# Channel attention: part of the sum of exponentials moves from TensorE to accumulating DMAs

## The reference

```python
q = jnp.einsum('bchw,oc->bohw', x, w_q)
kwin = _unfold2d(kmap, 7)     # 49 shifted windows of the padded keys, plus rel_h or rel_w
vwin = _unfold2d(vmap, 7)
attn = jax.nn.softmax(q[..., None] * kwin, axis=-1)   # over the 49 taps
out = jnp.sum(attn * vwin, axis=-1)                   # each channel by itself
```

## Time and profile before

| what | value |
|---|---|
| runs of the kernel | 8085.47, 8098.6, 8104.42 us; median 8098.6 |
| span of the profiled execution | 8087.0 us |
| instructions | 141762 |
| mean granted TensorE clock | 0.979 |

### The profile page before, as it was taken

The page is one execution under the profiler, slowest core; times in us unless marked ns, Lnnn a source line. Parts: engine busy times, 40 slices in busy tenths (PEclk is TensorE's granted clock), DMA queues, the critical chain, the costliest instruction groups (busy, mean ns, idle before and its releaser), DMA issues. The chain is left out here.

```text
span 8087.0 us, 141762 instructions
## 1 busy us (share of the span) xinstructions
PE 7551.7 (93%) x55106; PEld 6507.3 (80%) x55106; DVE 5845.1 (72%) x8981; ACT 3601.8 (45%) x6912; POOL 4566.7 (56%) x2002
## 2 busy tenths in 40 slices
PE   5999998999997998799999999999999999997999
PEld 4777776789997775588888888888888888886899
DVE  5666665334442555798998999999999989996664
ACT  3556554333332332345445454545545454554222
POOL 3555552033331001588777887878878787886232
PEclk9999998999998999899999999999999999998999
DMA  3111114855557772100000000000000000002452
GB/s 144 57 60 66 56 62 137 277 152 146 148 146 215 220 206 85 25 19 19 24 21 21 18 18 26 18 20 19 20 27 18 15 21 24 23 12 79 144 163 81
DMA packets 633017, 617.20 MB, mean 76 GB/s; under 512 B 465525, under 2 KB 498421, under 8 KB 627174
## 3 DMA queue, kind: packets, MB, share of 16 engines
q1 hardware_dynamic: 581318, 483.44, 21.5%
q0 software_dynamic: 33856, 96.69, 3.3%
q10 hardware_dynamic: 17376, 30.54, 1.0%
HBM read 397.01 MB, written 193.76 MB: 73 GB/s over the span
## 5 line engine op out<-in xcount | busy, mean ns | idle before, releaser
L1892 POOL TENSOR_TENSOR e_ev<-e_se,e_v 128x2048 f32<-128x2048 f32 (+1 forms) x896 | 3307.9, 3712 | 858.9 <-ACT e_se L1845 856.5
L1845 ACT ACTIVATE e_se<-e_stage 128x512 f32<-128x512 f32 x3136 | 1868.5, 598 | 2038.3 <-PE e_stage L1677 1991.5
L1991 DVE SCALAR_TENSOR_TENSOR e_stage<-e_k,e_rl,e_qp 128x512 f32<-128x512 f32 x3136 | 2299.7, 746 | 250.1 <-ACT e_se L1845 199.3
L1684 PE MATMUL e_pe_sum<-e_ident,e_se 128*128 128x128 f32 x12544 | 1888.5, 273 | 16.4 <-ACT e_se L1845 12.2
L1684 PE MATMUL e_pv_sum<-e_ident,e_ev 128*128 128x128 f32 x12544 | 1881.1, 273 | 0.5 <-POOL e_ev L1892 0.5
L1684 PEld LDWEIGHTS e_pe_sum<-e_ident,e_se 128*128 128x128 f32 x12544 | 1556.7, 140 | 261.3 <-ACT e_es L1833 21.8
L1677 PE MATMUL e_stage<-e_top,e_minus 128*128 128x512 f32 x3136 | 1513.4, 483 | 163.1 <-DVE e_stage L1991 160.9
L1684 PEld LDWEIGHTS e_pv_sum<-e_ident,e_ev 128*128 128x128 f32 x12544 | 1483.0, 141 | 205.7 <-issue 203.7
L911 POOL DMA_DIRECT2D agg<-c_ot x384 | 334.6, 874 | 880.6 <-ACT c_ot L989 771.0
L403 POOL TENSOR_TENSOR a_pr<-a_pr,a_rden 128x480 f32<-128x480 f32 x512 | 494.6, 987 | 547.2 <-DVE a_rden L636 547.2
L1677 PEld LDWEIGHTS e_stage<-e_top,e_minus 128*128 128x128 f32 x3136 | 598.2, 191 | 219.6 <-DVE e_stage L1991 185.2
(11 more groups left out here) (175 smaller groups left out, 11663.9 us busy)
## 6 DMA issues: line engine op xcount, KB each, us to landing
qkv<-b_ot SPq DMA_DIRECT2D x120, 512.0 KB, 5.9
c_xt<-qkv SPq DMA_DIRECT2D x384, 160.0 KB, 3.8
agg<-c_ot POOLq DMA_DIRECT2D x384, 160.0 KB, 2.5
f_ws<-in_L_w_sets SPq DMA_DIRECT2D x32, 1152.0 KB, 8.0
a_xb<-in_x SPq DMA_DIRECT2D x24, 768.0 KB, 5.1
a_xr<-in_x SPq DMA_DIRECT2D x32, 512.0 KB, 3.8
x<-a_xr SPq DMA_DIRECT2D x32, 512.0 KB, 2.7
b_xc<-x SPq DMA_DIRECT2D x32, 512.0 KB, 6.0
```

The costliest lines, as they stand in the source:

```text
L1684: last = nc.tensor.matmul(acc[:, c * PART:(c + 1) * PART], lhsT=src[:, c * PART:(c + 1) * PART], rhs=ident[:], is_transpose=True, start=j ...
L1845: nc.scalar.activation(se[(t * K2 + o) % NSE][:, i], stage[:, bank_of(t, j), :], ACT.Exp)\
L1892: nc.gpsimd.tensor_tensor(split(ev[(t * NG2 + g) % NEV][:, 0:size]), split(se[(t * K2 + o) % NSE][:, i:i + size]), window(v[h], h, u, o, i ...
L1991: nc.vector.scalar_tensor_tensor(rows(stage[:, bank_of(t, j), :]), win, rl[:, h, o:o + 1], rows(qp[:]), ALU.add, ALU.mult).then_inc(multip ...
```

## The change

Two accumulators `acc` of four tap tiles (4 x 512 elements on 128 partitions, 1 MB) take turns from tile to tile. ACT writes the exponentials of taps 0 to 3 of row 0 into the accumulator in place of `se`. After POOL has weighed both parts of row 1, it issues a DMA that adds the first four taps of that row (in `se`) onto the accumulator, in SBUF; likewise for rows 2, 3 and 4, each after the one before has landed. PE no longer adds the first four taps of rows 0 to 4 (20 tiles). In place of them it adds the four tiles of the accumulator, one each at taps 44, 45, 46 and 47, after it has waited at tap 44 for the DMA of row 4. So PE adds 33 tiles (29 directly, four gathered) in place of 49; the weighted sums stay as they were. ACT's waits on buffers follow: those for gathered parts wait for the DMA's landing.

```diff
+        acc = [sb(f"acc{u}", [PART, ROW_PARTS[0][1], TPX]) for u in range(2)]
...
+        gathered = sem("gathered")
...
+        GATHERED = (1, 2, 3, 4)
+        NACC = ROW_PARTS[0][1]
+        DIRECT = [j for j in range(NTAP) if j % K2 >= NACC or j // K2 not in (0, *GATHERED)]
+        NES = len(DIRECT) + NACC
+        ACC_AT = (44, 45, 46, 47)
...
+        def exps(t, j, taps=None):
+            o, i = divmod(j, K2)
+            buf = acc[t % 2] if o == 0 and i < NACC else se[(t * K2 + o) % NSE]
+            return buf[:, i] if taps is None else buf[:, i:i + taps]
+        def sums_made(n, t, j):
+            return tiles(n, t, NES, sum(d <= j for d in DIRECT) + sum(a < j + E_LAG for a in ACC_AT))
+        def gathers(n, t, o):
+            return 16 * tiles(n, t, len(GATHERED), sum(r <= o for r in GATHERED))
...
             def sum_exponential(n, t, j, first=False):
-                o, i = divmod(j, K2)
-                if j == 0 and (t or not first):
+                if j == DIRECT[0] and (t or not first):
                     pe.wait_ge(e_taken, tiles(n, t, 1, 0))
                 pe.wait_ge(exp_done, tiles(n, t, NTAP, j + 1))
-                add_up(pe_sum, se[(t * K2 + o) % NSE][:, i], j).then_inc(e_summed, 1)
+                add_up(pe_sum, exps(t, j), j == DIRECT[0], j == DIRECT[-1]).then_inc(e_summed, 1)
+            def sum_gathered(n, t, i):
+                if i == 0:
+                    pe.wait_ge(gathered, gathers(n, t, K2))
+                add_up(pe_sum, acc[t % 2][:, i], False, False).then_inc(e_summed, 1)
...
                 shift(n, t, j)
-                if t * NTAP + j >= E_LAG or not first:
+                if (t * NTAP + j >= E_LAG or not first) and before(t, j, E_LAG)[1] in DIRECT:
                     sum_exponential(n, *before(t, j, E_LAG), first=first)
+                if j in ACC_AT:
+                    sum_gathered(n, t, ACC_AT.index(j))
...
+                if j == 0 and (t >= 2 or not first):
+                    act.wait_ge(e_summed, tiles(n, t - 2, NES, NES))
+                elif i == start and j:
+                    lag = NSE * K2
+                    if part_of(j) == 0 and before(t, j, lag)[1] == 0:
+                        lag *= 2
+                    if t * NTAP + j >= lag or not first:
+                        t0, j0 = before(t, j, lag)
+                        if part_of(j) == 0 and j0 // K2 in GATHERED:
+                            act.wait_ge(gathered, gathers(n, t0, j0 // K2))
+                        else:
+                            act.wait_ge(e_summed, sums_made(n, t0, j0 + size - 1))
+                        act.wait_ge(weighted, tiles(n, t0, NG2, group_of(j0) + 1))
...
+            def gather(n, t, o):
+                if o == GATHERED[0]:
+                    pool.wait_ge(weighted, tiles(n, t, NG2, 1))
+                else:
+                    pool.wait_ge(gathered, gathers(n, t, o - 1))
+                flat = lambda x: x.rearrange("p i n -> p (i n)")
+                pool.dma_start(flat(acc[t % 2][:]), flat(se[(t * K2 + o) % NSE][:, 0:NACC]), accum_op=ALU.add).then_inc(gathered, 16)
...
                     for g in range(NG2):
                         weigh(n, t, g, first=n == 0)
+                        if g % 2 and g // 2 in GATHERED:
+                            gather(n, t, g // 2)
```

More of the change, by code:

```diff
@@ L1569, in bank_lag, with part_of @@
             return 2 if t * NTAP + j in (1, TPB * NTAP - 1) else NST
+        def exps(t, j, taps=None):
[6 more added lines that the diff above has]
+            return 16 * tiles(n, t, len(GATHERED), sum(r <= o for r in GATHERED))
+        def part_of(j):
+            return group_of(j) % len(ROW_PARTS)
         def group_of(j):
@@ L1679, in shift, with add_up @@
                                  skip_group_check=True).then_inc(shifted, 1)
-            def add_up(acc, src, j):
+            def add_up(total, src, opens_, closes):
                 for c in range(NBLK2):
-                    last = nc.tensor.matmul(acc[:, c * PART:(c + 1) * PART], lhsT=src[:, c * PART:(c + 1) * PART],
-                                            rhs=ident[:], is_transpose=True, start=j == 0 and c == 0,
-                                            stop=j == NTAP - 1, skip_group_check=True)
+                    last = nc.tensor.matmul(total[:, c * PART:(c + 1) * PART], lhsT=src[:, c * PART:(c + 1) * PART],
+                                            rhs=ident[:], is_transpose=True, start=opens_ and c == 0,
+                                            stop=closes, skip_group_check=True)
                 return last
             def sum_exponential(n, t, j, first=False):
-                o, i = divmod(j, K2)
-                if j == 0 and (t or not first):
+                if j == DIRECT[0] and (t or not first):
                     pe.wait_ge(e_taken, tiles(n, t, 1, 0))
                 pe.wait_ge(exp_done, tiles(n, t, NTAP, j + 1))
-                add_up(pe_sum, se[(t * K2 + o) % NSE][:, i], j).then_inc(e_summed, 1)
+                add_up(pe_sum, exps(t, j), j == DIRECT[0], j == DIRECT[-1]).then_inc(e_summed, 1)
[3 more added lines that the diff above has]
+                add_up(pe_sum, acc[t % 2][:, i], False, False).then_inc(e_summed, 1)
             def sum_weighted(n, t, j, first=False):
@@ L1704, in sum_weighted @@
                     pe.wait_ge(weighted, tiles(n, t, NG2, g + 1))
-                add_up(pv_sum, ev[(t * NG2 + g) % NEV][:, i], j).then_inc(v_summed, 1)
+                add_up(pv_sum, ev[(t * NG2 + g) % NEV][:, i], j == 0, j == NTAP - 1).then_inc(v_summed, 1)
             def back(n, t, copies=0, near_=0):
@@ L1828, in take_e_sums @@
             def take_e_sums(n, t):
-                act.wait_ge(e_summed, tiles(n, t, NTAP, NTAP))
+                act.wait_ge(e_summed, tiles(n, t, NES, NES))
                 if t > 0 or n:
@@ L1838, in exponential @@
                 start, size = ROW_PARTS[g % 2]
[L1839 to L1843, removed]
+                if j == 0 and (t >= 2 or not first):
[11 more added lines that the diff above has]
+                        act.wait_ge(weighted, tiles(n, t0, NG2, group_of(j0) + 1))
                 act.wait_ge(shifted, tiles(n, t, NTAP, j + 1))
-                nc.scalar.activation(se[(t * K2 + o) % NSE][:, i], stage[:, bank_of(t, j), :], ACT.Exp)\
-                    .then_inc(exp_done, 1)
+                nc.scalar.activation(exps(t, j), stage[:, bank_of(t, j), :], ACT.Exp).then_inc(exp_done, 1)
             def step(n, t, j, first=False, final=False):
@@ L1892, in weigh @@
                 nc.gpsimd.tensor_tensor(split(ev[(t * NG2 + g) % NEV][:, 0:size]),
-                                        split(se[(t * K2 + o) % NSE][:, i:i + size]),
+                                        split(exps(t, o * K2 + i, size)),
                                         window(v[h], h, u, o, i, size), ALU.mult).then_inc(weighted, 1)
+            def gather(n, t, o):
[5 more added lines that the diff above has]
+                pool.dma_start(flat(acc[t % 2][:]), flat(se[(t * K2 + o) % NSE][:, 0:NACC]), accum_op=ALU.add).then_inc(gathered, 16)
             for x in (xb, *k, *v, near, pair):
```

## The result

The changed kernel took 8252.35 us (median), 1.0193 of the kernel before (95% interval 1.0178 to 1.0207): 156 us slower, where 118 us faster was forecast. The time lies inside the stated range, at its upper end; the direction was wrong.

A forecast was written before the change was run, and what follows sets the result against it. Three engines nearly full, PE first: odd tiles PE-bound, even ones not wholly. Odd tiles 2.0 us less, even 1.6: 3.6 to 3.7 a pair over 32 pairs, 118 us off 8098.6, giving 7980 us; range 7,800 to 8,270.

The forecast's parts named there:

- a loop that leaves 57.7 us for an odd tile: From one landing of gather 4 to the next, through PE's wait at tap 44: 57.7 us, 2.0 less than 59.7.
- The removed sums: On PE, 16 of 49 tile sums a tile go: 16 x 0.43 = 6.9 us, 440 us were PE alone the limit.
- POOL then does five rows of taps with three issues: 39.2: Odd tile, POOL's first multiply to the end of row 4: 5 x 7.36 + 2.4 = 39.2 us.
- the sign that POOL's idle on exponentials would shrink by more than half: Listed sign in the stage: POOL's wait for exponentials, 589.5 us between 4000 and 7000 us, shrinks by more than half.
- taps 29 to 34 at 0.66: Even tile, DVE's products after tap 28, at 0.66 us each, put product 34 at 51.6 us after the landing.
- The 43.6 us up to tap 28: Even tile, DVE's first product to that of tap 28: 43.6 us, DVE almost without a gap, unchanged by PE's relief.
- the first product 4.0 after the landing: Even tile, DVE's first product after PE's landing point: 3.2 us before, 4.0 with two gathered sums in the way.
- The half microsecond for the clock: Added to each tile's time, 0.5 us for the granted clock falling after PE's stand at tap 44.
- The landing, D = 6.8 us: Time for a 1 MB gather to land: 6.8 us, by two reads and a little more; bounds 4.0 and 9.2.
- The deciding point, 8.2 us: Landing time over which gathers are too slow, POOL waiting before each of three gathers and PE longer.
- The rival that came true (slower, 0.32): Gathers too slow, landing over 8.2 us; at 9.2 us +5.4 a pair, +173, about 8,270 us; chance 0.32.
- The lost DVE time: DVE's small tensor_scalar locked out by POOL: at most 141 us over 72 instructions, growth likelier, counted in a half microsecond.

The follow-up runs named there:

- no_gathers: The changed kernel without its DMAs and PE's wait for them, the first four taps of rows 1 to 4 left out of the sum: 8036.68 us, 0.9935.
- light DVE: The changed kernel without gathers or their wait, and 24 of 34 instructions of DVE's bounds chain per half band made eight times smaller: 7928.97 us, 0.9798.
- half_bytes: The changed kernel with gathers of two of the four tap tiles, 512 KB in place of 1 MB: 8049.13 us, 0.9952.
- next_tile: The changed kernel with the four gathered sums moved from taps 44 to 47 to taps 2 to 5 of the next tile, copy and inversions later: 7991.5 us, 0.9876.
- rows_2_to_5: The kernel with gathered sums at the next tile's taps 2 to 5, with rows 2 to 5 gathered in place of 1 to 4: 8242.07 us, 1.0184.
- next_tile_no_gathers: The kernel with the four sums at the next tile's taps 2 to 5, without its DMAs and the wait for them: 7953.22 us, 0.9821.

## Why the prediction was wrong

The mechanism that lost the time was in the prediction: the wait at tap 44, in order ahead of the shifts of 45 to 48, the DVE that starves behind it, the clock that falls after a long stand. It stood there as a loop that leaves 57.7 us for an odd tile. PE's stand itself came out as forecast: on the mean 2.9 us in odd tiles, where some 3 were written, and 1.5 in even ones. What failed is the rest of the loop, which was longer than worked out. Here it is in its parts, each the mean of 28 tiles of its kind:

| stretch of the loop, us | forecast | measured |
|---|---|---|
| odd tile: landing to POOL's first multiply | 10.7 | 10.96 |
| from there to the end of row 4 | 39.2 | 43.34 |
| to the landing, issue included | 6.8 | 7.33 |
| even tile: landing to DVE's first product | 4.0 | 5.64 |
| from there to the end of row 4 | 54.9 (58.9 - 4.0) | 58.80 |
| to the landing, issue included | 6.8 | 7.22 |
| allowed for clock and jitter in both | 2.0 | in the rows above |
| pair | 124.4 | 133.3 |

*The removed sums* were counted rightly: 4096 matmuls less. I then let PE's relief reach the end of row 4, in both kinds of tile, and it does not.

*Odd tile, "POOL then does five rows of taps with three issues: 39.2".* This is the step that failed first. It made POOL full from row 0 to row 4. In the odd tile shown, POOL began row 0 at 4987.10 and ended row 4 at 5031.53 (the multiplies of its timeline):

```profile
4987.10 4.19 POOL L1932 TENSOR_TENSOR e_ev<-e_acc,e_v 128x2048 f32<-128x2048 f32 x1 [0.80 <-ACT e_acc L1886]
4991.32 3.19 POOL L1932 TENSOR_TENSOR e_ev<-e_se,e_v 128x1536 f32<-128x1536 f32 x1
4997.09 7.36 POOL L1932 TENSOR_TENSOR e_ev<-e_se,e_v 128x2048 f32<-128x2048 f32 x2 [2.58 <-ACT e_se L1886]
5004.39 0.85 POOL L1943 DMA_DIRECT2D e_acc<-e_se  x1
5005.56 7.38 POOL L1932 TENSOR_TENSOR e_ev<-e_se,e_v 128x2048 f32<-128x2048 f32 x2 [0.32 <-ACT e_se L1886]
5014.96 0.87 POOL L1943 DMA_DIRECT2D e_acc<-e_se  x1 [2.02 <-DMA e_acc<-e_se]
```

That is 44.4 us. In it POOL waited 2.58 for exponentials and 2.02 for its own first gather, which landed later than the median 7.4; another 0.95, for the third, came behind row 4. The kernel before already waited for exponentials in this stretch. In the odd tile of the earlier trace rows POOL began row 0 at 4919.50 and ended row 4 at 4964.33, a third of the way through the 22.09 us from 4956.97: 44.8 us.

```profile
4919.50 7.35 POOL L1892 TENSOR_TENSOR e_ev<-e_se,e_v 128x2048 f32<-128x2048 f32 x2 [0.65 <-ACT e_se L1845]
```

On the mean the stretch took 43.7 us before and 43.3 after; the forecast took all of its waits away. Most of the miss is not the gathers' doing: in no_gathers the stretch still took 41.7, though five rows of multiplies without an issue need 36.8. DVE's work holds part of that: with light DVE it took 40.3. So the sign that POOL's idle on exponentials would shrink by more than half failed too: 589.5 us before, and 461.5 and 43.0 (on `se` and on `acc`) after, 504.5 together.

*Even tile, "taps 29 to 34 at 0.66".* In the even tile shown DVE's product of tap 28 starts at 5088.95 and that of tap 34 at 5096.44: 7.5 us, not 4.0. DVE's timeline has three reductions in it, and PE's the two projections at taps 29 and 30, which the change does not touch (0.88 us each by the distance of starts). Both stand in the kernel before as well, where these six taps took 8.4 us on the mean; I had subtracted the sums and forgotten the rest:

```profile
5088.95 0.74 DVE L2042 SCALAR_TENSOR_TENSOR e_stage<-e_k,e_rl,e_qp 128x512 f32<-128x512 f32 x1
5089.60 0.95 DVE L1997 TENSOR_REDUCE e_near<-e_pair 128x192 f32<-128x768 f32 x1
...
5096.44 0.76 DVE L2042 SCALAR_TENSOR_TENSOR e_stage<-e_k,e_rl,e_qp 128x512 f32<-128x512 f32 x1 [0.80 <-ACT e_se L1886]
```
```profile
5092.51 1.04 PE L1690 MATMUL e_pj<-e_xb,e_wt 128*128 128x512 f32 x2
5093.39 0.60 PE L1708 MATMUL e_pv_sum<-e_ident,e_ev 128*128 128x128 f32 x4
5093.74 0.48 PE L1701 MATMUL e_stage<-e_top,e_minus 128*128 128x512 f32 x1
5094.06 1.04 PE L1690 MATMUL e_pj<-e_xb,e_wt 128*128 128x512 f32 x2
```

The 43.6 us up to tap 28 held (43.8 on the mean), though DVE was busy for 39.57 of them in the kernel before, so not "almost without a gap".

*Even tile, the first product 4.0 after the landing.* It took 5.76 us in the tile shown (5039.47 to 5045.23). In it the granted clock was 0.57, and the four transposes of one sum took 0.87 (5039.47 to 5040.34) in place of 0.43. The half microsecond for the clock was the term that was too small; I had costed the two more sums at full clock.

In both kinds of tile the end of row 4, counted from DVE's first product, came only 0.2 us (odd) and 0.5 us (even) earlier than in the kernel before, on the mean, and PE came to tap 44 earlier by 1.8 and 1.4 us. The earlier arrival became a longer stand.

*The landing, D = 6.8 us,* measured 7.4 (half_bytes 4.6): a term 0.6 too small. Its rate was forecast well, 2.8 us for 512 KB against 2.6. The rule that was cited from the Trainium skill, Collectives: The Full Stack, section "The bandwidth ceiling: the fold count and why AG ≠ RS ≠ AR", agrees with the two sizes: twice the plain 1.3 us per 512 KB. That two reads are the reason is shown by no run here. *The deciding point, 8.2 us,* fell with the steps above. Between half_bytes (4.6 us, 0.9952) and the changed kernel (7.4 us, 1.0193) the ratio crosses one; a straight line through the two, an estimate, crosses at 5.2 us. The rival that came true (slower, 0.32) blamed the same gathers, but its condition, a landing over 8.2 us with POOL waiting before each of three gathers, was not met: POOL waited for its gathers only 23.2 us in 3 ms. That the time came out near the rival's 8,270 us, and so inside the range, is luck. (The rival's own sum gives 5.5 us a pair, not 5.4, which changes nothing.)

*POOL's issue,* 0.8 us, was 0.87. *The lost DVE time* of the small tensor_scalar did not grow: its mean from 3600 to 7300 us was 1346 ns in the changed kernel against 1432. *DVE's busy time* stayed, but its share fell to 86%, not 93%. *PE's busy time* in the stage fell by 197 us, not by 440; in no_gathers it fell by 273 (3662.3 us). A lone matmul of a sum shows 0.27 us, four in a stream 0.60, and at the clock of 0.57 up to 1.09. So what stands apart or runs at the lower clock counts longer; how much each makes was not taken apart. *Clock:* 0.96, above the 0.95 named.

In sum, against the kernel before: relief in its place -0.65% (no_gathers), the gathers without a wait +0.55% (measured in next_tile), and the rest, some 2.0%, the wait that the gathers bring at tap 44. The last is a difference of the others: gathers cost 2.6% where their sums stand at tap 44 (1.0193 against 0.9935) and 0.55% where they stand in the next tile. half_bytes and rows_2_to_5 support it: with a shorter landing nearly all of it goes, and with a wait at the other place it comes back. What follows from the wait, DVE's starving and the lower clock among it, is in the 2.0% and was not parted.

## What to carry to other kernels

Work taken off the fullest engine comes out only at the taps where that engine was the bound: look at each stretch, with every other instruction that stays there, before multiplying a saving by its count. When a forecast makes an engine full, first read how long the same stretch takes now and what ends its waits. A result that arrives by DMA should be used where its wait can't stop anything else; here the same change went from 1.9% slower to 1.2% faster by adding the gathered tiles seven steps later, at taps where PE has no exponential sum of its own. When a wait is predicted, ask what sets the arrival of both sides: relief moves the waiting engine forward, and not what it waits for.

## What the runs showed of the hardware

- An issue of an accumulating DMA on POOL shows 0.87 us, but the next multiply starts 0.60 after it (5014.96 to 5015.56) and a pair of them then takes 7.69 us in place of 7.36.
- Gathers slow some other transfers: a store of 512 KB landed in 6.0 us, against 2.7 and 2.7 in no_gathers. A load of 512 KB stayed at 3.9 in all three kernels.
- In next_tile POOL is busier, and DVE's small tensor_scalar waited through more than one POOL instruction. POOL's two multiplies ended at 4953.64, the tensor_scalar at 4953.69 (first POOL's timeline, then DVE's, of next_tile). Its mean there, from 3600 to 7300 us, was 1797 ns, against 1475 in next_tile_no_gathers: over the 62 in that stretch 20 us of DVE time, so part of the 45 us that the gathers still cost in next_tile may lie here; that was not tried apart.

```profile
4946.01 7.63 POOL L1935 TENSOR_TENSOR e_ev<-e_se,e_v 128x1536 f32<-128x1536 f32 x2
```
```profile
4948.59 5.10 DVE L1985 TENSOR_SCALAR e_pair<-e_k 128x48 f32<-128x48 f32 x1 [0.79 <-ACT e_k L1853]
```
